# Scan of a Mamba block beside its mixture of experts: another wait for zz of state 0, front projections placed ahead of expert tiles

## The reference, cut to what matters

```python
xz = x @ in_proj_w                          # 128 -> 2 x 256: xb and zb
xb = silu(causal_conv(xb, conv_w, taps=4) + conv_b)
zb = silu(zb)
x_dbl = xb @ x_proj_w                       # dt (16), B (16), C (16)
dt = softplus(dt @ dt_proj_w + dt_proj_b)
decay = exp(dt[..., None] * A)              # 256 channels x 16 states
inp = dt[..., None] * B[:, :, None, :] * xb[..., None]
h = decay * h + inp                         # over the 512 tokens
y = sum over states of h * C
out = (y + xb * D) * zb @ out_proj_w
# x = x + ga * out; then h = layernorm(x) * (1 + cb) + sb
for e in range(8):
    ye = relu(h @ w1[e] + b1[e]) @ w2[e] + b2[e]     # taken where expert e is chosen
```

## Time and profile before

| | |
|---|---|
| median of 3 runs | 3730.88 us (3724.39 to 3731.93) |
| the profiled execution | 3736.28 us, its span 3734.5 us |
| mean granted TensorE clock | 0.914 of full |
| PE / PEld busy | 2956.4 us (79%) / 2164.0 us (58%) |
| DVE busy | 2804.6 us (75%) |
| ACT busy | 1952.3 us (52%) |
| POOL busy | 888.7 us (24%) |

### The profile page before, as it was taken

The page is one execution under the profiler, slowest core; times in us unless marked ns, Lnnn a source line. Parts: engine busy times, 40 slices in busy tenths (PEclk is TensorE's granted clock), DMA queues, the critical chain, the costliest instruction groups (busy, mean ns, idle before and its releaser), DMA issues. The chain is left out here.

```text
span 3734.5 us, 53471 instructions
## 1 busy us (share of the span) xinstructions
PE 2956.4 (79%) x15912; PEld 2164.0 (58%) x15912; DVE 2804.6 (75%) x4814; ACT 1952.3 (52%) x4744; POOL 888.7 (24%) x590
## 2 busy tenths in 40 slices
PE   2387888888888888888888958888888888888886
PEld 1164465556555655565566726666666666666665
DVE  3999889888988998898889336666666666666664
ACT  3466667667665766576667434333333333333332
POOL 0443333334333333333333000111111111111111
PEclk6598999989898999999899989999999999999988
DMA  2000000000000000000000010000000000000000
GB/s 100 7 4 14 16 19 3 18 15 15 6 18 15 3 18 15 18 3 18 15 13 4 16 70 14 17 16 24 15 15 15 15 15 15 15 15 15 15 8 10
DMA packets 49771, 64.31 MB, mean 17 GB/s; under 512 B 3584, under 2 KB 36416, under 8 KB 49184
## 3 DMA queue, kind: packets, MB, share of 16 engines
q1 hardware_dynamic: 47392, 54.93, 4.6%
q10 hardware_dynamic: 2304, 8.46, 0.6%
HBM read 41.78 MB, written 21.60 MB: 17 GB/s over the span
## 5 line engine op out<-in xcount | busy, mean ns | idle before, releaser
L787 POOL TENSOR_TENSOR acc<-acc,zz 128x1024 f32<-128x1024 f32 x256 | 607.8, 2374 | 1114.1 <-DVE h L1101 1010.2
L1101 DVE TENSOR_TENSOR_SCAN h<-dec,u 128x1024 f32<-128x1024 f32 x256 | 585.4, 2287 | 13.2 <-issue 4.8
L916 PEld LDWEIGHTS bank<-one_sb,hid 128*128 128x128 f32 x4096 | 485.6, 194 | 20.8 <-issue 11.2
L864 PE MATMUL bank<-S,pick_sb 96*128 96x512 bf16 x512 | 215.1, 425 | 350.4 <-DVE zz L1110 225.2
L916 PE MATMUL bank<-one_sb,hid 128*128 128x128 f32 x4096 | 484.8, 277 | 0.0
L622 ACT ACTIVATE dec<-dt,aneg 128x512 f32<-128x512 f32 (+1 forms) x512 | 341.4, 723 | 75.3 <-DVE h L1101 60.0
L158 POOL TENSOR_SCALAR n_ve<-n_mv 128x4 f32<-128x4 f32 x96 | 54.4, 567 | 1355.6 <-DVE n_mv L141 1355.6
L864 PEld LDWEIGHTS bank<-S,pick_sb 96*128 96x128 bf16 x512 | 50.4, 99 | 561.2 <-DVE zz L1110 275.5
L1110 DVE TENSOR_TENSOR zz<-h,bank 128x1024 f32<-128x1024 f32 x256 | 312.5, 1221 | 58.5 <-POOL acc L787 49.8
L1094 DVE TENSOR_TENSOR u<-dtx,bank 128x1024 f32<-128x1024 f32 x256 | 309.8, 1210 | 1.9 <-issue 1.6
L654 ACT ACTIVATE hid<-banks,one_sb 128x512 f32<-128x512 f32 x304 | 209.1, 694 | 96.3 <-PE bank L916 71.5
(11 more groups left out here) (265 smaller groups left out, 6990.9 us busy)
## 6 DMA issues: line engine op xcount, KB each, us to landing
kv_dram<-Gs ACTq DMA_DIRECT2D x16, 516.5 KB, 3.1
kvl<-kv_dram SPq DMA_DIRECT2D x16, 516.5 KB, 3.5
xs<-in_x SPq DMA_DIRECT2D x16, 256.0 KB, 2.8
x<-in_x SPq DMA_DIRECT2D x16, 256.0 KB, 2.9
x_dram<-x SPq DMA_DIRECT2D x16, 256.0 KB, 2.1
h_dram<-hT SPq DMA_DIRECT2D x16, 256.0 KB, 2.0
h<-h_dram SPq DMA_DIRECT2D x16, 256.0 KB, 2.6
x2s<-x_dram SPq DMA_DIRECT2D x16, 256.0 KB, 2.7
```

The lines of the kernel that those rows point to most:

```text
L787: pool.tensor_tensor(acc[:, :, :], acc[:, :, :], zz[:, k % 2, :, :], ALU.add)\
L864: pe.matmul(banks[which][:, :], pick_sb[:, at:at + 1].to_broadcast([96, P]), S[0:96, :], start=True, stop=True).then_inc((cbc if which els ...
L916: last = pe.matmul(bank1(f"down{e}")[:, j * D:(j + 1) * D], hid[:, e % 2, f, j * P:(j + 1) * P], w2[:, e, f, :], start=(f == 0), stop=(f = ...
L1101: dve.tensor_tensor_scan(h[:, :, :].rearrange("p g t -> p (g t)"), dec[:, k % 2, :, :].rearrange("p g t -> p (g t)"), u[:, :, :].rearrange ...
```

## The change

- `weigh` gets the batch before, `last`. zz of state 0 waits for 15 additions of the batch before, up to state 14, instead of all 16. State 1 still waits for all 16, the others as before.
- TensorE issues `in_x` (slots 8, 9) and `x_proj` right after the broadcast of B, ahead of the slot's further tiles; `x_proj` is in slot 11 instead of 12, the dt projections in 12 and 13 instead of 13 and 14, at the end of the slot as before.
- ScalarE has `keep_x` and `split_x` behind the slot's first relus (UPS_PRE) and ahead of the other relus and the decay, `split_x` in slot 11 instead of 12. `silu_x` is at the end of slot 10 instead of 11; `round_rest` and the first magnitude at the end of 12 instead of 13, the second magnitude 13 instead of 14, the softplus 14 instead of 15.
- VectorE has the convolutions in slots 9 and 10 instead of 10 and 11, `split_mid` in 12 instead of 13, `split_low` in 13 instead of 14.

```diff
--- before.py
+++ after.py
@@ -444,7 +444,7 @@
             TAKES = {slot + 1: e for slot, e in DOWNS.items() if slot + 1 < SLOTS}
             EXPS = {8: 0, 9: 1, 10: 2, 11: 3}
             XIN = {8: 0, 9: 1}
-            CONV = {10: 0, 11: 1}
+            CONV = {9: 0, 10: 1}
 
 
 
@@ -722,6 +722,11 @@
                             if b is not None:
                                 for q in UPS_PRE.get(slot, ()):
                                     relu(q, b)
+                            if n is not None:
+                                if slot in XIN:
+                                    keep_x(XIN[slot], n)
+                                if slot == 11:
+                                    split_x(n)
                             if y is not None:
                                 for m in KEYS_POST.get(slot, ())[:1]:
                                     key_square(m, y)
@@ -745,18 +750,14 @@
                             if n is not None:
                                 if slot == 7:
                                     modulate1(n)
-                                if slot in XIN:
-                                    keep_x(XIN[slot], n)
-                                if slot == 11:
+                                if slot == 10:
                                     silu_x(n)
                                 if slot == 12:
-                                    split_x(n)
-                                if slot == 13:
                                     round_rest(n)
                                     magnitude(0, n)
+                                if slot == 13:
+                                    magnitude(1, n)
                                 if slot == 14:
-                                    magnitude(1, n)
-                                if slot == 15:
                                     softplus(n)
                         if n is not None:
                             keep_split(a, n)
@@ -990,6 +991,11 @@
                                     ups(q, b, s)
                             if a is not None and 0 < k + 1 < NS:
                                 spread(k + 1, 0, a)
+                            if n is not None:
+                                if slot in XIN:
+                                    in_x(XIN[slot], n, s)
+                                if slot == 11:
+                                    x_proj(n, s)
                             if y is not None and slot == 2:
                                 turn3(y, s)
                             if b is not None and slot == 2:
@@ -1011,17 +1017,13 @@
                                     key_tile(m, y, s)
                             if a is not None and slot in (5, 6):
                                 in_z(slot - 5, a, s)
-                            if n is not None and slot == 12:
-                                x_proj(n, s)
                             if b is not None and slot in DOWNS:
                                 downs(DOWNS[slot], b, s)
                             if n is not None:
                                 if slot == 7:
                                     turn1(n, s)
-                                if slot in XIN:
-                                    in_x(XIN[slot], n, s)
-                                if slot in (13, 14):
-                                    dt_proj(slot - 13, n, s)
+                                if slot in (12, 13):
+                                    dt_proj(slot - 12, n, s)
                         if n is not None:
                             spread(0, 0, n, a)
                         if y is not None:
@@ -1103,10 +1105,13 @@
                                                u[:, :, :].rearrange("p g t -> p (g t)"), 0.0,
                                                ALU.mult, ALU.add).then_inc(scan.sem, 1)
 
-                    def weigh(k, a):
+                    def weigh(k, a, last):
                         dve.wait_ge(*scan(a, k + 1))
                         dve.wait_ge(*cbc(a, k + 1))
-                        dve.wait_ge(*accum(a, k - 1 if k >= 2 else 0))
+                        if k > 0:
+                            dve.wait_ge(*accum(a, k - 1))
+                        elif last is not None:
+                            dve.wait_ge(*accum(last, NS - 1))
                         dve.tensor_tensor(zz[:, k % 2, :, :], h[:, :, :], mid(banks[1][:, :], G), ALU.mult)\
                            .then_inc(z_ok.sem, 1)
 
@@ -1249,15 +1254,15 @@
                                     norm_apply(dve, L1, xs, n)
                                 if slot in CONV:
                                     convolve(CONV[slot], n)
+                                if slot == 12:
+                                    split_mid(n)
                                 if slot == 13:
-                                    split_mid(n)
-                                if slot == 14:
                                     split_low(n)
                             if n is not None and slot == NS:
                                 softplus(n)
                             if a is not None and k >= 0:
                                 scans(k, a)
-                                weigh(k, a)
+                                weigh(k, a, b)
                             if b is not None:
                                 if slot in TAKES:
                                     take(TAKES[slot], b)
```

## The result

The changed kernel takes 3739.61 us, median of 13 runs (3735.02 to 3745.51), the kernel before 3728.89, median of 13 runs (3721.06 to 3735.87). The ratio is 1.0030, 95% interval 1.0021 to 1.0039: slower by 11 us, where 14 were forecast. The profiled execution took 3745.51, with a span of 3743.7.

The account below looks back on a forecast made before the run. The first sweep was taken to go at VectorE's pace. Per step, front +2.7, zz -2.65, out projection -0.2: 129.3 against a mean of 127.9, +18 over 13 steps, +14 with the ends: 3744 us, range 3703 to 3768.

Parts of the forecast that it names:

- the gain of zz: VectorE's zz of state 0 no longer waits for state 15's addition: 2.65 us gained, 15 times; bounds 2.3 and 3.28.
- the front: First-sweep convolutions, projections, splits and softplus moved a slot earlier: together a step 2.7 us longer; bounds 0.0 and +3.1.
- the signs: Trace features listed as showing the forecast right or wrong, among them norm_apply of slot 2 near 2 us.
- The four waits of the earlier trace: VectorE waits in the first sweep: zz for addition 36.4 us, dt for logarithm 30.0, Sn for first half 29.0, rounded rest 7.3.
- The x projection: TensorE, slot 11: idle 4.4 us for silu where it was 2.31, ahead of two up tiles and a down tile.
- (c): Rival: in_x in slot 8 also idles 1.4 us and lowers the clock; +1.3 a step, 3761; chance 0.18 with (d).
- the likeliest one: The forecast itself: losses of the front over the gain of zz, 3744 us; chance 0.50.
- The clock's price: Low TensorE clock at slot 11's x projection and down tile: 2.7 us taken, bounds 0 and 3.07.
- ScalarE's queue: From relu 20, ScalarE's work takes 7.9 us to split_low, which waits some 4 us; dt follows 16.2 later.
- (a): Rival: TensorE's clock stays full, the front costs 0.0 a step; 3709 us, or 3727 if half the steps; chance 0.28.
- (b): Rival: front hidden altogether, no relu or down tile holds anything up; 8.45 us gained 14 times, 3613; chance 0.04.
- (d): Rival: the earlier zz delays state 15's addition, which now decides yz; 0.6 us a step more; chance 0.18 with (c).

Follow-up runs that it names:

- the rounding ahead: Changed kernel with ScalarE's `round_rest` moved from the end of slot 12 to right behind `split_x` in slot 11: 3715.14 us, ratio 0.9974 to the kernel before.
- silu ahead: Changed kernel with `silu_x` moved to the head of ScalarE's slot 10, ahead of its relus: 3623.58 us, ratio 0.9717 to the kernel before.
- the four matmuls: Changed kernel with four more matmuls ahead of the x projection, which overwrites their result, to keep the clock up: 3720.92 us, ratio 0.9977 to the kernel before.
- the two matmuls on the kernel before: Kernel before with two more matmuls ahead of the x projection, which overwrites their result: 3707.01 us, ratio 0.9946.
- the two matmuls with zz: Kernel before with two filling matmuls ahead of the x projection and the edit of zz: 3663.37 us, ratio 0.9829.
- the projection behind the tiles: Changed kernel with `x_proj` put behind slot 11's up tiles and down tile on TensorE: 3665.34 us, ratio 0.9839 to the kernel before.

## Why the prediction was right

**Time and sign.** 3744 us was forecast and 3739.61 measured, +14 against +11. The cause was the forecast one: the gain of zz (2.63 a step, 41 us in all) is more than spent by the front (55 us alone). That the time came so close is partly luck, as the terms below show. (The last addition, 3730.88 + 14, gives 3744.9 and was written as 3744.)

**The edit of zz.** 2.65 against 2.63. The earlier trace rows decided it: without the meeting of norm_apply and addition I would have taken 3.28. norm_apply ended 0.86 us after the addition here (1195.76 against 1194.90), as in the earlier trace rows. It took 1.60 us; the signs named 2, the sum 1.73. The Trainium skill's page "SBUF — State Buffer", section "Who interferes with whom", has one of the two wait for the other's whole instruction. By an estimate from that rule norm_apply would end 1.11 us after the addition instead of 0.86: the trace agrees that it is held up, and not fully with the size. That the edit alone would bring only 15 us was not foreseen, neither in the prediction nor in the first expectation.

**What bounds the kernel.** The four waits of the earlier trace rows were called nearly all of VectorE's idle time. They are 102.7 of its 158.5 us from 330 to 1800, two thirds. No term of the forecast hung on it.

**The x projection.** Idle 4.4 forecast, 4.2 to 4.7 measured; 3.77 us at low clock. It came at 22.2 us after u of slot 9 instead of 21.3, because rival (c) happened as well: in_x idle for 1.40 us (1.4 forecast), the clock down, a down tile of 5.02. In 12 of the 13 full steps in_x runs at low clock (1.91 to 2.05 us, 1.02 before); its down tile then takes about 5.0 us in four, 4.0 in four and 3.73 in the rest. So (c) was given 0.18 as a case of its own, but it belonged to the likeliest one, and its price of 17 us did not appear: its 0.9 us a step came, its full price of the clock did not. From u of slot 9 to dt the step took 55.6 us, 55.2 forecast; the stretch from dt to u of slot 9 took 73.4 where 76.95 - 2.65 = 74.3 follow from the forecast. That 0.9 cancelled the other: in the step of before, VectorE's Ek waited 0.99 us for ScalarE's Gs (L678) there, and here it doesn't. The prediction kept that wait.

**The clock's price** was mis-sized: from the projection's start to that of the down tile 5.49 us, 2.2 over the 3.3 of full clock, where I took 2.7; the down tile itself was at full clock again (3.73). So relu 20 came 9.3 after the projection's start instead of 9.8.

**ScalarE's queue.** 7.9 forecast from relu 20 to split_low, 8.0 measured; then 16.1 to dt, 16.2 forecast; a wait of 4.15, 4 forecast; no wait before dt. The next limit was taken to be the softplus; the experiment with the rounding ahead shows its wait come up again, but with 0.7 us a step only, beside the broadcasts.

**The sum.** The front cost 0.6 + 2.6 = 3.2 a step over the mean of before, where 1.4 + 2.65 = 4.1 were forecast; part of this is the clock's price. The other terms were wrong in size, and their errors cancelled half: full steps +8 (+18 forecast); batch 1's step, dt to dt, +1.8 (-1 forecast); the last, dt to yz, -4.3 (-2.65); the rest of the profile, from the last yz on, +4.3 (0 forecast); what stands ahead of batch 1's step, -0.7 (0 forecast). From the last yz on no edit was made. This part took 1668.1 us before, 1672.4 after, 1670.2 with silu ahead and 1678.8 with the four matmuls; whether this is the run or follows from the first sweep stays open, and so one profile tells such small differences only roughly.

**The rivals.** (a), a clock that stays up, is refuted by all 16 projections of the trace (3.64 to 3.78 us); made true by four matmuls, it gives 3720.92, by sign the side that was named (3709 was its price). (b), a hidden front, is refuted, but it was the prize: 3613 was its price, and silu ahead gets to 3623.58. (d) didn't show: the addition of state 15 starts 16.25 us after dt, 16.24 before.

## What to carry to other kernels

An instruction moved ahead in an in-order queue must have its input ready there: follow its producer back through the other engines' queues first. Here silu stood behind three relus that waited for a down tile, and its consumer went ahead of the tiles that feed the next relus. Moving the producer into a gap of its own engine won 116 us; its consumer's place ahead of the tiles, without that, cost 71 to 74, more than everything else in the change gained.

## What was not expected of the hardware

The length of a step is not the sum of its waits alone. Late in the first sweep four kernels with different waits have dt to dt 126.3 us within 0.05 (the edit of zz alone, the four matmuls, the rounding ahead, the two matmuls on the kernel before), two have 122.9 (the two matmuls with zz, the projection behind the tiles). In the kernel before steps of 125.7, 128.0, 128.8 and 129.5 follow each other, as the projection takes 1.98, 3.4 or 3.78 us after the same idle time of 2.3: it costs the clock in some steps and not in others. The granted clock doesn't fall at a fixed point of an idle time either: in the steps shown it falls 1.7 us into the one ahead of the projection before, and in the changed kernel 2.5 us into the one ahead of the projection, but only 0.4 us into the one ahead of in_x (an idle time of 1.33 us stood 1.6 us before that). The windows of TensorE there, with the granted clock in the last place but two:

```profile
1245.20:1245.60 0.40, 0.31 (x2) 1.00 0.00 0
1245.60:1246.00 0.40, 0.00 (x0) 0.87 0.00 0
1246.00:1246.40 0.40, 0.00 (x0) 0.50 0.00 0
```

A kernel 2.6 us a step shorter, the edit of zz alone, met the low clock in each step and showed 15 of 41 us. I read the one as the cause of the other, since the same edit shows 43.6 with the clock held up; why steps settle at common lengths was seen and not taken apart.
